# Slot tables of an edge-placing pass: the running sum on VectorE and bf16 parts in place of fp32 products

## The chip, the cores and the metric

One core of a Trainium2 chip runs the whole program; the other cores are idle. The metric is the device time of one execution in microseconds (us). TensorE (PE) multiplies matrices, VectorE (DVE) and ScalarE (ACT) work elementwise, GpSimd (POOL) issues the indirect transfers, SyncE (SP) the plain ones. Each engine runs its own list of instructions in order, and they meet through semaphores.

## The reference

The inputs are 6250 nodes with 128 features and 100000 edges, each with a source and a destination node. Two graph layers follow one another: an attention layer with 8 heads, whose softmax runs over the edges of one source node, and an edge MLP with a sum over the edges of each source; each is followed by a residual and a layer norm.

```python
q, k, v = x @ Wq.T + bq, x @ Wk.T + bk, x @ Wv.T + bv      # (6250, 8, 16)
scores  = sum(q[src] * k[dst], -1) / 4 + edge_attr_8
weights = softmax of scores over the edges with the same src
out     = segment_sum(v[src] * weights, dst) @ Wo.T + bo
x = layernorm(x + out)
h = silu(concat(x[src], x[dst], edge_attr_2) @ eW1 + eb1);  e = silu(h @ eW2 + eb2)
x = layernorm(x + silu(concat(x, segment_sum(e, src)) @ nW1 + nb1) @ nW2 + nb2)
```

## The kernel before

The nodes are cut into 49 windows of 128 lanes, so node n is lane n % 128 of window n / 128. The edges lie in 784 tiles of 128, one edge to a partition. Before anything is computed on them the edges are sorted by source: a first pass (`count_nodes`) counts the edges of each node, and the pass that the change touches (`place_and_project`) gives every edge its slot in a list padded by window and sends its record of 16 floats to that slot in DRAM. After it the records are read back (`load_records`), and scores, softmax, weighted sums, the projection, the edge MLP and the node MLP follow, one block after the other. Each block ends with all engines meeting.

The placing pass takes PG = 8 tiles at a time, 98 steps g in all, two (b = 0 and 1, doubly buffered) to an iteration i. For a step:

- `nodes` (DVE, helper line 229) makes 8 one-hots over the 128 lanes, `windows` (DVE, line 223) 8 one-hots over the WC = 50 window columns. Both are bf16 and are stored with the tile index innermost, so one tile's one-hot is read with a stride of 8 elements.
- `turn` (PE, L588) transposes the 8 lane one-hots, `turned` (ACT, L549 and L550) copies them out of PSUM twice, as bf16 and as fp32.
- `gram` (PE, L596) multiplies each transposed one-hot with itself: which edges of a tile share a lane. `earlier` (DVE, L459) masks this to the edges that come earlier in the tile.
- `count` (PE) builds the table of next free slots by lane and window, for each of the 8 tiles and for the one after them: L607 writes the running table 9 times by an fp32 product with the identity (450 columns), then L610 adds the one-hot counts of tile k to the tables k+1 to 8 (8 products of 400 down to 50 columns). `keep` (ACT, L541) copies it out.
- `slots_of` (PE) looks up each edge's entry: L622, an fp32 product of the turned one-hot with the kept table (50 columns, issued as two passes), and L623, a bf16 product that adds the earlier edges of the same tile.
- `finish` (DVE, L487 to L519) masks the result with the window one-hot (L487), sums it (L491), works out the row of the record in short operations on 8 columns (L495 to L517) and copies the record (L519). On b = 1 it also splits the projected q and v rows into three bf16 parts and stores them (L470 to L481).
- `send` (POOL, L652) issues 8 indirect transfers, one for each tile. `finish` waits for those of step g - 2 before it writes the same buffers (`s_sent`).
- On b = 0, `project` (PE, L580 and L581) makes one window's q, k and v rows: an fp32 product of a row of ones with the bias (384 columns, one row deep) and one of x with the weights.

The order on each engine is written out by hand. In step g, PE does slots(g), count(g+1), gram(g+1), project, turn(g+2). DVE does earlier(g+1), nodes(g+2), finish(g), windows(g+2). ACT does keep(g+1), the copies of the projection, turned(g+2). ACT first issues 20 transfers that zero the sums (L535).

## Time and profile before

| | us |
|---|---|
| median of 3 runs | 6396.11 (6384.83 to 6405.34) |
| the profiled execution | 6388.47 |
| its span, first to last instruction | 6386.7 |
| first record transfer of the placing pass starts | 189.73 |
| last one starts | 1488.43 |
| reading back starts | 1500.28 |

The placing pass is about a fifth of the span. Over the whole span PE is 63% busy, POOL 57%, DVE 37% and ACT 19%. Overlapping durations count once in a busy time. In a row of the timeline, the bracket holds how long the engine sat idle before the instruction and what ended that.

### The profile page before, as it was taken

The numbers are of one execution on the slowest core, as the hardware profiler recorded it, in microseconds if no ns is written. First come the engines' busy times: TensorE is split into PE (matmuls) and PEld (weight loads), VectorE is DVE, ScalarE is ACT, GpSimd is POOL, SyncE is SP. The second block draws the span as 40 slices with busy tenths as digits, with TensorE's granted clock in tenths as the row PEclk, the third lists the DMA queues.
The fourth block names the chain that finished last, engine by engine and source line by source line (L and its number), as shares of the span: only waits on it lengthen the run. The fifth ranks groups of instructions, "written<-read, shape, count | busy, mean of one in ns | idle before, by whom it ended". The sixth has DMA issues, their size and how long they took to land. (4 is left out here: it accounts for less than half of the span.)

```text
span 6386.7 us, 92237 instructions
## 1 busy us (share of the span) xinstructions
PE 4045.0 (63%) x25409; PEld 3223.8 (50%) x25410; DVE 2370.2 (37%) x6387; ACT 1207.9 (19%) x2083; POOL 3663.4 (57%) x3321
## 2 busy tenths in 40 slices
PE   6899998993433343322666566666255778877786
PEld 4566555552222222212555555555235667766674
DVE  6344434442222222258232222222243334343344
ACT  0222222220111110101111111111022333333332
POOL 0455555555666666631888888888404555555551
PEclk9555555555565555555777777777567888888888
DMA  2100000002111111100444444444511111111111
GB/s 111 54 10 10 10 10 10 10 10 68 43 42 44 43 41 44 42 22 4 36 35 35 35 36 35 35 36 36 104 58 34 37 37 37 38 37 37 37 37 53
DMA packets 278676, 238.39 MB, mean 37 GB/s; under 512 B 57255, under 2 KB 246759, under 8 KB 278246
## 3 DMA queue, kind: packets, MB, share of 16 engines
q0 software_dynamic: 198144, 170.19, 17.2%
q1 hardware_dynamic: 77604, 54.50, 2.8%
q10 hardware_dynamic: 2880, 13.11, 0.5%
q8 instruction: 25, 0.41, 0.0%
q14 instruction: 23, 0.18, 0.0%
HBM read 143.89 MB, written 93.71 MB: 37 GB/s over the span
## 5 line engine op out<-in xcount | busy, mean ns | idle before, releaser
L1075 POOL DMA_INDIRECT sums_dram<-we_merged_rows,we_idx x832 | 1286.3, 1546 | 477.8 <-DVE we_idx L1127 226.2
L1670 POOL DMA_INDIRECT ed_bg<-b_rows_dram,ed_idx x832 | 792.4, 952 | 669.8 <-DVE ed_idx L1678 442.3
L652 POOL DMA_INDIRECT records_dram<-rec_out,row_idx x784 | 768.0, 980 | 577.3 <-DVE rec_out L519 297.8
L751 POOL DMA_INDIRECT sc_k<-k_rows_dram,sc_idx x832 | 799.8, 961 | 470.4 <-issue 248.8
L1195 PE MATMUL ps_merged<-we_rows,we_same_dst 128*128 128x129 f32 x1664 | 359.3, 383 | 588.6 <-issue 429.5
L1195 PEld LDWEIGHTS ps_merged<-we_rows,we_same_dst 128*128 128x128 f32 x1664 | 307.8, 276 | 623.6 <-issue 613.8
L853 PE MATMUL ps_q<-tab,sc_oht 128*128 x2496 | 372.0, 263 | 373.5 <-issue 369.4
L1815 PE MATMUL ps_ed_s<-ed_ohf,ed_efs 128*128 128x128 f32 x1664 | 432.8, 417 | 188.6 <-ACT ed_efs L1755 126.4
L853 PEld LDWEIGHTS ps_q<-tab,sc_oht 128*128 128x128 bf16 x2496 | 249.8, 103 | 495.8 <-issue 442.1
L779 DVE TENSOR_TENSOR sc_prods<-ps_q,sc_k 128x1024 f32<-128x1024 f32 x104 | 127.2, 1223 | 925.9 <-remote 884.9
L1815 PEld LDWEIGHTS ps_ed_s<-ed_ohf,ed_efs 128*128 128x128 f32 x1664 | 335.8, 226 | 235.1 <-issue 193.2
L1114 DVE SCALAR_TENSOR_TENSOR we_firsts<-we_merged_rows,lane_unmark,two_marks 128x4 f32<-128x4 f32 x208 | 46.2, 222 | 1067.2 <-ACT we_merged_rows L1149 1067.2
L459 DVE TENSOR_TENSOR place_earlier<-ps_gram,tri 128x512 bf16<-128x512 f32 x196 | 126.2, 686 | 771.2 <-PE ps_gram L596 657.3
L622 PE MATMUL ps_slots<-place_table,place_oh_tf 128*128 128x50 f32 x1568 | 405.6, 408 | 0.0
L622 PEld LDWEIGHTS ps_slots<-place_table,place_oh_tf 128*128 128x128 f32 x1568 | 398.7, 328 | 0.6 <-issue 0.6
L1149 ACT ACTIVATE we_merged_rows<-ps_merged 128x516 f32<-128x516 f32 x208 | 125.0, 601 | 1288.9 <-DMA sums_dram<-we_merged_rows,we_idx 1274.2
L843 PE MATMUL ps_oht<-identb,sc_oh 128*128 128x128 bf16 x832 | 100.8, 286 | 415.4 <-ACT sc_oht L816 202.5
L1174 PE MATMUL ps_dst_row<-ident,we_dsts 128*128 128x128 f32 x1664 | 351.5, 383 | 0.0
L1693 DVE TENSOR_TENSOR ed_hs<-ps_z,ed_bg 128x512 f32<-128x512 f32 x208 | 143.5, 690 | 546.3 <-remote 429.7
L1174 PEld LDWEIGHTS ps_dst_row<-ident,we_dsts 128*128 128x128 f32 x1664 | 337.1, 299 | 0.0
L610 PE MATMUL ps_table<-place_ohw,place_oh 128*128 128x400 bf16 (+7 forms) x784 | 332.5, 582 | 0.0
L1707 DVE TENSOR_TENSOR vals<-vals,ps_ed_s 128x128 f32 x832 | 238.9, 287 | 193.1 <-issue 99.2
(288 smaller groups left out, 7736.7 us busy)
## 6 DMA issues: line engine op xcount, KB each, us to landing
sc_k<-k_rows_dram,sc_idx POOLq DMA_INDIRECT x832
sums_dram<-we_merged_rows,we_idx POOLq DMA_INDIRECT x832
ed_bg<-b_rows_dram,ed_idx POOLq DMA_INDIRECT x832
sums_dram<-zero_rows ACTq DMA_DIRECT2D x20, 640.0 KB, 8.5
records_dram<-rec_out,row_idx POOLq DMA_INDIRECT x784
co_rows<-sums_dram SPq DMA_DIRECT2D x48, 256.0 KB, 3.9
records_dram<-rfill SPq DMA_DIRECT2D x16, 416.0 KB, 6.9
records<-records_dram SPq DMA_DIRECT2D x1, 6656.0 KB, 18.5
```

What stands on the lines that cost most here:

```text
L610: ins = pe.matmul(table[:, k + 1:PG + 1, :], ohl[:, b, :, k], ohw[:, b, :, k].unsqueeze(1).to_broadcast([P, PG - k, WC]), start=False, sto ...
L622: pe.matmul(slots[b][:, k, :], ltf[:, b, k, :], kept[:, b, k, :], start=True, stop=False)
L652: pool.indirect_dma_start(c.rec_rows, bass.IndirectOffsetOnAxis(ap=idx[:, b, j:j + 1], axis=0), out[:, b, j, :], None, bounds_check=SLOTS ...
L751: pool.indirect_dma_start(kg[:, r, k * F:(k + 1) * F], None, c.k_dram[:, :], bass.IndirectOffsetOnAxis(ap=idx[:, r, k:k + 1], axis=0)).the ...
L853: ins = pe.matmul(psq[b][:, k * F:(k + 1) * F], oht[:, b, k, :], c.tab[:, j, bass.ds(win[k] * F, F)], start=(j == 0), stop=(j == 2))
L1075: pool.indirect_dma_start(c.acc_dram[k][:, :], bass.IndirectOffsetOnAxis(ap=idx[:, r, k:k + 1], axis=0), rows[:, r, k, 0:F], None, compute ...
L1174: ins = pe.matmul(psd[:, k * P:(k + 1) * P], dst[:, r, k:k + 1].to_broadcast([P, P]), c.ident[:, :], start=True, stop=True)
L1195: ins = pe.matmul(merged[b][:, k, 0:F + 1], same[:, b, k, :], con[:, b, k, :], start=True, stop=True)
L1670: pool.indirect_dma_start(bg[:, r, k * F:(k + 1) * F], None, c.b_dram[:, :], bass.IndirectOffsetOnAxis(ap=idx[:, r, k:k + 1], axis=0)).the ...
L1693: dve.tensor_tensor(h[:, b, :], psz[b][:, :], bg[:, r, :], ALU.add).then_inc(s_zs, 1)
L1707: dve.tensor_tensor(acc, acc, pss[r % 2][:, k * P:(k + 1) * P], ALU.add).then_inc(s_add, 1)
L1815: ins = pe.matmul(pss[b][:, k * P:(k + 1) * P], ef[:, b, k, :], ohf[:, b, :, k], start=True, stop=True)
```

## The change

- `keep` moves from ACT to DVE. PE no longer writes the running table: its count products start their own accumulation (`start=(k == 0)`, 400 columns instead of 450), and DVE adds the table before the step to the sums in PSUM (fp32, `kept`). DVE then splits the kept table into two bf16 parts (`kb`): a copy to bf16 and a subtraction.
- `slots_of` does two bf16 products with these parts in place of the fp32 one. ACT's fp32 copy of the turned one-hots is gone; the bf16 one is now doubly buffered.
- The window one-hots are stored tile by tile (contiguous blocks of 50), made by `blocks_onehot`; count and slots_of read them without a stride. They are made inside `finish`, right after the masking.
- The bias is split into three bf16 parts once, ahead of the loop (`bias_rows_of_qkv`), and added by one bf16 product of ones with a tile whose first three rows hold the parts. It is loaded to all partitions.
- The order: PE does count(g+1), gram(g+1), slots(g), project, turn(g+2); DVE does nodes(g+2), keep(g+1), earlier(g+1), finish(g) with windows(g+2) inside.

```diff
+def blocks_onehot(dve, c, e, t0, out):
+
+    return dve.tensor_tensor(out, c.iotab[:, 0:WC, 0].unsqueeze(1).to_broadcast([P, PG, WC]),
+                             e.hi[:, bass.ds(t0, PG)].unsqueeze(2).to_broadcast([P, PG, WC]), ALU.is_equal)
+
...
-        ohw = sb("place_ohw", [P, 2, WC, PG], BF16)
-        lt = sb("place_oh_t", [P, PG, P], BF16)
-        ltf = sb("place_oh_tf", [P, 2, PG, P], F32)
+        ohw = sb("place_ohw", [P, 2, PG, WC], BF16)
+        lt = sb("place_oh_t", [P, 2, PG, P], BF16)
+        kb = sb("place_table_parts", [P, 2, 2, PG, WC], BF16)
...
+        bias = sb("b_qkv", [P, 3 * F], F32)
+        bp = sb("b_qkv_parts", [P, 3, 3 * F], BF16)
+        bk = sb("b_qkv_rows", [P, 3 * F], BF16)
...
                 def windows(i, b):
                     g = 2 * i + b
+                    wait_count(dve, s_msk, g - 1)
+                    blocks_onehot(dve, c, e, g * PG, ohw[:, b]).then_inc(s_ohw, 1)
+
+                def keep(i, b):
+
+                    g = 2 * i + b
                     wait_count(dve, s_slots, g - 1)
-                    wait_count(dve, s_msk, g - 1)
-                    windows_onehot(dve, c, e, g * PG, ohw[:, b]).then_inc(s_ohw, 1)
+                    dve.wait_ge(s_hist, g + 1)
+                    wait_count(dve, s_tab, 2 * g)
+                    before = e.start[:, :] if isinstance(g, int) and g == 0 else kept[:, 1 - b, PG, :]
+                    dve.tensor_copy(kept[:, b, 0, :], before).then_inc(s_tab, 1)
+                    dve.tensor_tensor(kept[:, b, 1:PG + 1, :], pstab[:, 0:PG * WC].rearrange("p (k w) -> p k w", w=WC),
+                                      before.unsqueeze(1).to_broadcast([P, PG, WC]), ALU.add).then_inc(s_tab, 1)
+                    dve.wait_ge(s_tab, 2 * g + 2)
+                    dve.tensor_copy(kb[:, b, 0], kept[:, b, 0:PG, :]).then_inc(s_parts, 1)
+                    dve.wait_ge(s_parts, 2 * g + 1)
+                    dve.tensor_tensor(kb[:, b, 1], kept[:, b, 0:PG, :], kb[:, b, 0], ALU.subtract).then_inc(s_parts, 1)
...
                     g = 2 * i + b
                     win = i if b == 1 else None
                     dve.wait_ge(s_slots, g + 1)
-                    dve.tensor_tensor(own[:, :, :], slots[b], ohw[:, b].rearrange("p w k -> p k w"), ALU.mult).then_inc(s_msk, 1)
+                    dve.tensor_tensor(own[:, :, :], slots[b], ohw[:, b], ALU.mult).then_inc(s_msk, 1)
+                    dve.wait_ge(s_msk, g + 1)
+                    ahead, half, there = pair_at(i, b, 2)
+                    if there:
+                        windows(ahead, half)
                     if win is not None:
                         part(win, 0)
-                    dve.wait_ge(s_msk, g + 1)
                     dve.tensor_reduce(slot[:, :], own[:, :, :], AX_X, ALU.add).then_inc(s_red, 1)
...
                 def step(i, b):
-                    for by, work in ((1, earlier), (2, nodes), (0, finish), (2, windows)):
+                    for by, work in ((2, nodes), (1, keep), (1, earlier), (0, finish)):
                         at, half, there = pair_at(i, b, by)
                         if there:
                             work(at, half)
+                    if isinstance(i, int) and i == -1:
+                        windows(0, b)
+                    if isinstance(i, int) and i == -1 and b == 1:
+                        bias_rows_of_qkv()
+
+                def bias_rows_of_qkv():
+
+                    dve.wait_ge(s_w, 96)
+                    n = 0
+                    for j in range(3):
+                        dve.tensor_copy(bp[:, j, :], bias[:, :]).then_inc(s_bias, 1)
+                        n += 1
+                        dve.wait_ge(s_bias, n)
+                        if j < 2:
+                            dve.tensor_tensor(bias[:, :], bias[:, :], bp[:, j, :], ALU.subtract).then_inc(s_bias, 1)
+                            n += 1
+                            dve.wait_ge(s_bias, n)
+                    dve.tensor_scalar(bk[:, :], bp[:, 0, :], c.ident[:, 0:1], None, ALU.mult).then_inc(s_bias, 1)
+                    for j in (1, 2):
+                        n += 1
+                        dve.wait_ge(s_bias, n)
+                        dve.scalar_tensor_tensor(out=bk[:, :], in0=bp[:, j, :], scalar=c.ident[:, j:j + 1],
+                                                 in1=bk[:, :], op0=ALU.mult, op1=ALU.add).then_inc(s_bias, 1)
...
-                def keep(i, b):
-                    g = 2 * i + b
-                    wait_count(act, s_slots, g - 1)
-                    act.wait_ge(s_hist, g + 1)
-                    act.activation(kept[:, b].rearrange("p k w -> p (k w)"), pstab[:, 0:(PG + 1) * WC],
-                                   ACT.Copy).then_inc(s_tab, 1)
-
                 def turned(i, b):
                     g = 2 * i + b
                     act.wait_ge(s_tr, g + 1)
-                    wait_count(act, s_gram, g)
                     wait_count(act, s_slots, g - 1)
-                    act.activation(lt[:, :, :].rearrange("p k n -> p (k n)"), pst[:, :], ACT.Copy).then_inc(s_lt, 1)
-                    act.activation(ltf[:, b].rearrange("p k n -> p (k n)"), pst[:, :], ACT.Copy).then_inc(s_lt, 1)
+                    act.activation(lt[:, b].rearrange("p k n -> p (k n)"), pst[:, :], ACT.Copy).then_inc(s_lt, 1)
...
                 def project(win):
+                    pe.wait_ge(s_bias, 8)
                     pe.wait_ge(s_x, 16 * win + 16)
                     wait_count(pe, s_qv, win)
                     wait_count(pe, s_k, win)
-                    pe.matmul(psx[:, 0:3 * F], one[:, :], bias[:, :], start=True, stop=False)
+                    pe.matmul(psx[:, 0:3 * F], c.ones[:, :], bk[:, :], start=True, stop=False)
...
                 def count(i, b):
 
 
                     g = 2 * i + b
-                    table = pstab[:, 0:(PG + 1) * WC].rearrange("p (k w) -> p k w", w=WC)
-                    before = e.start[:, :] if isinstance(g, int) and g == 0 else kept[:, 1 - b, PG, :]
+                    table = pstab[:, 0:PG * WC].rearrange("p (k w) -> p k w", w=WC)
                     pe.wait_ge(s_ohw, g + 1)
-                    wait_count(pe, s_tab, g)
-                    pe.matmul(table, c.ident[:, :], before.unsqueeze(1).to_broadcast([P, PG + 1, WC]),
-                              start=True, stop=True)
+                    wait_count(pe, s_tab, 2 * g)
                     for k in range(PG):
-                        ins = pe.matmul(table[:, k + 1:PG + 1, :], ohl[:, b, :, k],
-                                        ohw[:, b, :, k].unsqueeze(1).to_broadcast([P, PG - k, WC]),
-                                        start=False, stop=True, skip_group_check=True)
+                        ins = pe.matmul(table[:, k:PG, :], ohl[:, b, :, k],
+                                        ohw[:, b, k, :].unsqueeze(1).to_broadcast([P, PG - k, WC]),
+                                        start=(k == 0), stop=True, skip_group_check=True)
                     ins.then_inc(s_hist, 1)
 
                 def slots_of(i, b):
                     g = 2 * i + b
                     pe.wait_ge(s_gm, g + 1)
-                    pe.wait_ge(s_tab, g + 1)
-                    pe.wait_ge(s_lt, 2 * g + 2)
+                    pe.wait_ge(s_parts, 2 * g + 2)
                     wait_count(pe, s_msk, g - 1)
                     for k in range(PG):
-                        pe.matmul(slots[b][:, k, :], ltf[:, b, k, :], kept[:, b, k, :], start=True, stop=False)
-                        ins = pe.matmul(slots[b][:, k, :], gm[:, b, k, :], ohw[:, b, :, k], start=False, stop=True)
+                        for j in range(2):
+                            pe.matmul(slots[b][:, k, :], lt[:, b, k, :], kb[:, b, j, k, :], start=(j == 0), stop=False)
+                        ins = pe.matmul(slots[b][:, k, :], gm[:, b, k, :], ohw[:, b, k, :], start=False, stop=True)
...
                 def step(i, b):
                     here = pair_at(i, b, 0)[2]
                     ahead, half, any_ahead = pair_at(i, b, 1)
                     later, later_half, any_later = pair_at(i, b, 2)
-                    if here:
-                        slots_of(i, b)
                     if any_ahead:
                         count(ahead, half)
                         gram(ahead, half)
+                    if here:
+                        slots_of(i, b)
                     if b == 0 and here:
                         project(i)
                     if any_later:
```

## Rows read from the trace of the kernel before

**Rows 1.** Busy time by engine; last are PE's granted clock, DMA share, GB/s.

```profile
400.00:800.00 400.00, 366.92 (x1565) 240.50 (x1565) 164.32 (x531) 83.77 (x135) 235.02 (x241) 0.51 0.05 10
```

**Rows 2.** The record copies on DVE: count, durations, first and last start.

```profile
L519 DVE COPY rec_out<-records x98: 217/227/232, 188.5 to 1474.4; 128x128 f32 x90, 128x128 f32<-128x128 f32 x8
```

**Rows 3.** Timeline of PE over one step: start, us, what ran.

```profile
811.17 1.07 PE L588 MATMUL ps_place_t<-identb,place_oh 128*128 128x128 bf16 x8 [2.06 <-DVE place_oh L229]
...
812.04 0.61 PE L622 MATMUL ps_slots<-place_table,place_oh_tf 128*128 128x50 f32 x2
...
816.13 1.82 PE L607 MATMUL ps_table<-place_table,ident 128*128 128x450 f32 x2
...
817.75 3.41 PE L610 MATMUL ps_table<-place_ohw,place_oh 128*128 128x400 bf16 x8
...
820.98 1.03 PE L596 MATMUL ps_gram<-place_oh_t 128*128 128x128 bf16 x8
...
821.94 1.64 PE L580 MATMUL ps_qkv<-b_qkv,one_row 1*128 1x384 f32 x2
...
823.52 1.65 PE L581 MATMUL ps_qkv<-w_qkv,xt 128*128 128x384 f32 x2
...
824.96 1.06 PE L588 MATMUL ps_place_t<-identb,place_oh 128*128 128x128 bf16 x8
```

**Rows 4.** Timeline of DVE: first and last instruction of two steps.

```profile
809.15 1.29 DVE L459 TENSOR_TENSOR place_earlier<-ps_gram,tri 128x512 bf16<-128x512 f32 x2 [8.69 <-PE ps_gram L596]
...
815.06 0.35 DVE L223 TENSOR_TENSOR place_ohw<-iota_by_tile,win_of 128x400 bf16<-128x400 bf16 x1
...
822.05 1.29 DVE L459 TENSOR_TENSOR place_earlier<-ps_gram,tri 128x512 bf16<-128x512 f32 x2 [6.63 <-PE ps_gram L596]
...
826.74 0.37 DVE L223 TENSOR_TENSOR place_ohw<-iota_by_tile,win_of 128x400 bf16<-128x400 bf16 x1
```

**Rows 5.** Timeline of POOL over its last 16 issues: first and last.

```profile
1469.30 0.97 POOL L652 DMA_INDIRECT records_dram<-rec_out,row_idx  x1 [1.95 <-issue]
...
1488.43 0.97 POOL L652 DMA_INDIRECT records_dram<-rec_out,row_idx  x1 [0.30 <-issue]
```

**Rows 6.** Transfers two us after that issue: DMA share and GB/s come last.

```profile
1491.00:1492.00 1.00, 0.00 (x0) 0.00 (x0) 0.00 (x0) 0.00 (x0) 0.00 (x0) 0.50 0.00 0
```

**Rows 7.** Groups of DVE in the stretch 400 to 2200, shapes kept apart.

```profile
L487 DVE TENSOR_TENSOR place_masked<-ps_slots,place_ohw 128x400 f32<-128x400 f32 x81 | 71.2, 878 | 2.8 <-PE ps_slots L623 2.8
...
L491 DVE TENSOR_REDUCE slot<-place_masked 128x8 f32<-128x400 f32 x81 | 45.9, 566 | 1.4
...
L470 DVE CAST qv_parts<-qv_rests 128x256 bf16<-128x256 f32 x82 | 23.5, 287 | 0.0
...
L475 DVE TENSOR_TENSOR qv_rests<-qv_rests,qv_parts 128x256 f32<-128x256 f32 x41 | 17.1, 417 | 0.0
...
L495 DVE CAST sloti<-slot 128x8 int32<-128x8 f32 x81 | 15.7, 194 | 1.4
```

**Rows 8.** Start of the pass: the timeline of ACT and POOL.

```profile
169.21 1.02 ACT L549 ACTIVATE place_oh_t<-ps_place_t 128x1024 bf16<-128x1024 bf16 x1 [64.12 <-issue]
...
189.73 1.22 POOL L652 DMA_INDIRECT records_dram<-rec_out,row_idx  x1 [45.65 <-DVE rec_out L519]
```

**Rows 9.** POOL's issues by group over the span; mean ns after the busy time.

```profile
L751 POOL DMA_INDIRECT sc_k<-k_rows_dram,sc_idx x832 | 799.8, 961 | 470.4 <-issue 248.8 <-DVE sc_idx L761 221.3 <-DVE sc_prods L779 0.3
...
L652 POOL DMA_INDIRECT records_dram<-rec_out,row_idx x784 | 768.0, 980 | 577.3 <-DVE rec_out L519 297.8 <-issue 279.5
```

**Rows 10.** Timeline of POOL and DVE where their instructions met.

```profile
397.20 0.68 DVE L229 TENSOR_TENSOR place_oh<-iota_by_tile,lane_of 128x1024 bf16<-128x1024 bf16 x1
397.25 1.48 POOL L652 DMA_INDIRECT records_dram<-rec_out,row_idx  x1 [0.30 <-issue]
...
1466.37 0.97 POOL L652 DMA_INDIRECT records_dram<-rec_out,row_idx  x1 [0.30 <-issue]
1466.89 0.45 DVE L495 CAST sloti<-slot 128x8 int32<-128x8 f32 x1
```

More of the change, by code:

```diff
@@ L401, in place_and_project @@
         w = sb("w_qkv", [P, 3 * F], F32)
-        bias = sb("b_qkv", [1, 3 * F], F32)
-        one = sb("one_row", [1, P], F32)
+        bias = sb("b_qkv", [P, 3 * F], F32)
+        bp = sb("b_qkv_parts", [P, 3, 3 * F], BF16)
+        bk = sb("b_qkv_rows", [P, 3 * F], BF16)
         xt = sb("xt", [P, P], F32)
@@ L560, in step @@
                 def step(i, b):
-                    ahead, half, there = pair_at(i, b, 1)
-                    if there:
-                        keep(ahead, half)
                     if b == 0 and (not isinstance(i, int) or 0 <= i < NW):
```

14 lines of the change are left out of this document (6 added, 8 removed).

## The prediction

> **What bounds the kernel now.** I read first the busy time of each engine in a stretch of the placing pass. PE is busy 367 of 400 us at a granted clock of 0.51, its lower level of 1.2 GHz, POOL 235, DVE 164 [rows 1]. The record copies on DVE give the pace: 98 of them, first to last (1474.4 - 188.5) / 97 = 13.26 us a step [rows 2]. The timeline of PE shows where this goes [rows 3]. A step with a projection is slots 4.09 us (812.04 to 816.13), the running table 1.62, count 3.23, gram 0.96, project 1.58 for the bias and 1.44 for x, turn 0.87: 13.8 us without a gap. A step without a projection has the first four and turn, and PE stands 2.06 us ahead of turn for the one-hots, which DVE makes only after it has had gram's result: 12.8. Their mean is the 13.3 of rows 2. So PE sets the pace, together with one hand-over to DVE in every second step. DVE waits 8.69 and 6.63 us for gram in the same two steps [rows 4], and a whole step of its own takes 6.26 us with the q and v parts and 5.06 without (first start to last end).
>
> The next limit is not DVE but POOL. Its last 16 issues stand back to back, with everything that they need long there: (1488.43 - 1469.30) / 15 = 1.275 us each, 0.97 of work and 0.30 of gap [rows 5]. A step has 8 of them, so POOL can't go below 10.20 us a step, 1000 us for the 784 issues. This is the number to compare all savings with.
>
> **PE, part by part.** The identity product goes: -1.62. Count keeps 1800 columns, which took 3.23 us with the stride (1.79 ns each); gram reads contiguous bf16 columns and takes 0.96 for 8 x 128 (0.94 ns each, loads and switch in it), so count costs 1.7. Slots go from 16 products (of which 8 in two passes) to 24 bf16 ones. Each needs a load of 128 columns; gram's pairs of load and product take 0.12, so 24 x 0.12 = 2.9 us; the upper bound is today's 4.09, as today too each tile has three loads. The bias goes from 1.58 to 384 x 0.94 ns = 0.36. New sum: 1.7 + 0.96 + 2.9 + 0.85 = 6.4, with a projection 8.2, mean 7.3 us. With slots and count not faster at all it is 4.09 + 3.23 + 0.96 + 0.85 + half of 1.8 = 10.0. At either end PE is under POOL's 10.20. The hand-over of 2.06 is gone too, as the lane one-hots are now the first thing in DVE's step.
>
> **ACT.** Two of its copies a step go. It waited for PE already, so this is worth nothing by itself; it lets go of gram and turn earlier.
>
> **DVE** gets work. keep is four instructions: a copy of 50 columns (at most the 0.23 of the record copy [rows 2], I take 0.2), an addition of 400 columns from PSUM (0.57 as the sum over 400 columns at L491, at most the 0.88 of L487, whose second input is strided), a copy to bf16 (0.29 for 256 columns at L470, 0.36 for 400), a subtraction (0.42 for 256 at L475, 0.57 for 400) [rows 7]: 1.7 us, at most 2.1. L487 loses its stride: 0.88 to 0.57, or no gain. The window one-hots were 0.36 us and now read one input with a stride and write 400 columns: 0.57 to 0.88, so +0.2 to +0.5, I take 0.35. Two steps: 6.26 + 5.06 + 2 x (1.7 - 0.3 + 0.35) = 14.8 us, bounds 14.3 and 16.6, against 20.4 at POOL. The order holds no circle that is longer: from the windows of g+1, PE needs 1.7 + 0.96 + 2.9 = 5.6 us to slots(g), while DVE has the rest of finish(g-1), nodes, keep and earlier to do, over 6 us, before it wants them.
>
> **POOL then sets the pace.** finish(g) waits for the transfers of step g - 2 before it writes the same buffers. After the last issue the transfers end within 2 us [rows 6], so the row indices of g are there some 8 us before POOL has done g - 1. DVE stands in this wait, and behind it stand the record copy, the tables and the one-hots of g+3, for which PE waits; but DVE needs 7.4 us from one such wait to the next and has 10.2. So POOL never starves, and PE and DVE idle.
>
> **Start and end.** Today ACT is held by its 20 issues and copies the first turned tiles at 169.21, and the first record goes at 189.73 [rows 8]. After: gram(0) as before, earlier(0) some 3.5 us behind that copy's start, to 172.7, windows(1) to 173.3, the bias rows on DVE (three copies of 384 columns at 0.36, two subtractions at 0.55, one product at 0.3, two fused operations at 0.55: 3.6 us with waits 3.9) to 177.2; nodes(2), keep(1), earlier(1), finish(0) take 0.7 + 1.7 + 1.3 + 3.2, PE's slots(0) are done at 178.3. The first record goes at about 185, 5 us earlier. The end is the same: reading back starts 10.9 us after the last issue ends.
>
> **POOL's price under load.** Today DVE works in large part while POOL waits. After, POOL never waits, so they meet more often. The trace shows both ways of it [rows 10]. L229, which reads two tensors from SBUF, began 0.05 us before an issue, and that issue took 1.48 in place of 0.97: it ended 0.85 after L229 had. A short cast that began 0.52 after an issue took 0.45, where the mean of its group is 0.19 [rows 7, 10], and ended with the issue. On average it is small: 980 ns against the usual 970 or so of rows 5; in the score pass, where POOL also runs in long stretches beside DVE, the like issues take 961 [rows 9]. After the change two steps hold, of operations with two inputs from SBUF, nodes 1.36, windows 1.2, the new subtraction 1.14, the rests of q and v 0.84 and six short fused ones 1.0, and of copies, casts and operations with a constant 0.4 + 0.72 + 1.4 + 0.46 + 0.87 + 0.57: 9.9 us in all, 4.95 a step. Today POOL meets chiefly L229, 0.68 a step, for about 8 x 9 ns. In proportion that is 0.07 x 4.95 / 0.68 = 0.5 us a step. Lower bound 0, upper bound all of the 4.95. I take 0.4: 10.6 us a step.
>
> The sum: 98 x 10.6 = 1039, from 185 to 1224, where 1489.4 stood: -265 us from the profiled execution's 6388.5, so 6123. That execution lies 7.6 us under the median of the runs shown, whose spread is 20 us; I say 6125. The floor, with nothing met, is 185 + 1000 = 1185: 6084. Changes under 0.3% (19 us) can't be told from none in this kernel.
>
> **The rivals.**
> *POOL is held up in part.* A third of DVE's 4.95 us a step lands on POOL: 11.8 us, 98 x 11.8 = 1156, -148: 6240. For it: DVE is released by POOL's own transfers, so its operations fall on a fixed phase, which may be a bad one. Against: the averages of rows 9.
> *DVE becomes the bound.* 19 short copies and operations in two steps, each lengthened by 0.26 as the one in rows 10, on the upper bound of 16.6: 21.5, 10.8 a step, -246: 6143. Against: the mean of 0.19 says how seldom it happens, though that is with POOL idle in part.
> *POOL is held up for all of it.* Every two-input operation, copy and cast of DVE stops the issue for its whole length: (20.4 + 9.9) / 2 = 15.1 us a step, 98 x 15.1 = 1480, +176: 6565. It decides from 3.06 us a step on, 0.38 on each issue; the worst single one in rows 10 is 0.51. Against: it needs nearly every operation to meet an issue at its sensitive moment.
> *PE and DVE in turn.* If count waited for windows and DVE for slots, a step would be 7.3 + 7.4 = 14.7 us: +139, 6530. The order above speaks against it.
> *The bf16 products and blocks are not faster.* PE at 10.0 stays hidden: 6125 as well.
>
> On holding up POOL the Trainium skill is stricter than the rows ("SBUF — State Buffer", Who interferes with whom): it calls the pair of ports that VectorE and GpSimd share an exclusive lock, taken for the whole instruction, by copies and casts in their two-port modes and by two-input operations against a GpSimd instruction that reads SBUF; the other side fully blocks. By that rule the third rival's 6565 is what would come; by the means, 980 ns against 970 undisturbed [rows 5, 9], it is 6125.
>
> **Chances.** POOL at 10.2 to 11.0: 0.68. Held up in part: 0.14. DVE the bound: 0.10. Held up in full 0.04, in turn 0.04. The first alone gives 6084 to 6165. For the range I add most of the second and the noise: 6080 to 6200. Faster 0.91, between 0.02, slower 0.07.
>
> **What would show it.** POOL: 0.30 us gaps marked as issue throughout, not waits for the record copy; 784 issues in 1000 to 1080 us, mean near 1.02 us. DVE idle ahead of the row index, for the transfers. PE's slots 2.9, count 1.7, bias 0.36 us, PE idle 30%. The forecast is wrong if POOL still waits for the record copy in every step, or if its mean goes over 1.15 us.

## The result

The changed kernel takes 6454.28 us (median of 4 runs, 6449.71 to 6467.23) where the kernel before takes 6400.73 on the same chip (4 runs, 6384.83 to 6406.03): ratio 1.0089, 95% interval 1.0076 to 1.0103. It is 54 us slower; 6125 was forecast. The profiled execution took 6454.73 us, 66 more than that of before. The placing pass holds nearly all of it: the last record transfer starts at 1547.0 where it was 1488.4 [rows 5].

The page's group of POOL's record transfers, to be set against L652 of before [rows 9], and the busy time of each engine in the stretch of rows 1:

```profile
L683 POOL DMA_INDIRECT records_dram<-rec_out,row_idx x784 | 797.7, 1017 | 718.4 <-DVE rec_out L543 481.6
```

```profile
400.00:800.00 400.00, 158.27 (x1393) 116.65 (x1391) 206.13 (x611) 36.48 (x70) 234.90 (x230) 0.57 0.05 10
```

PE fell from 367 of 400 us to 158, which is 5.5 us a step where 7.3 was forecast, and POOL's mean is 1017 ns, which is the forecast's. But POOL did no more in the stretch than before (234.90 us for 235), and over the pass it waited 481.6 us for the record copy in place of 297.8. No engine is busy for more than 59% of the time. The view of one line's instructions, for the transfers, gives the pace: from 183.2 to 1547.0, and without the last 7 issues (8.9 us) this is (1363.8 - 8.9) / 97 = 13.97 us a step. Worked out in the same way, before has 13.30.

```profile
L683 POOL DMA_INDIRECT records_dram<-rec_out,row_idx x784: 969/972/1602, 183.2 to 1547.0; - x196
```

**What a step looks like.** Timeline of POOL over one run of issues, and what follows it. Start, us, what ran; in brackets the idle time ahead and what ended it:

```profile
745.18 0.97 POOL L683 DMA_INDIRECT records_dram<-rec_out,row_idx  x1 [8.17 <-DVE rec_out L543]
746.45 0.97 POOL L683 DMA_INDIRECT records_dram<-rec_out,row_idx  x1 [0.30 <-issue]
...
754.91 0.97 POOL L683 DMA_INDIRECT records_dram<-rec_out,row_idx  x1 [0.30 <-issue]
756.19 1.34 POOL L683 DMA_INDIRECT records_dram<-rec_out,row_idx  x1 [0.30 <-issue]
...
765.49 0.97 POOL L683 DMA_INDIRECT records_dram<-rec_out,row_idx  x1 [0.30 <-issue]
772.83 0.97 POOL L683 DMA_INDIRECT records_dram<-rec_out,row_idx  x1 [6.36 <-DVE rec_out L543]
```

Sixteen issues, two steps' worth, without a gap, and then 6.4 us of nothing. PE's timeline over the same time, to be set against [rows 3]:

```profile
749.79 1.72 PE L642 MATMUL ps_table<-place_ohw,place_oh 128*128 128x400 bf16 x8 [3.33 <-DVE place_ohw L229]
751.35 1.04 PE L631 MATMUL ps_gram<-place_oh_t 128*128 128x128 bf16 x8
752.18 0.29 PE L654 MATMUL ps_slots<-place_table_parts,place_oh_t 128*128 128x50 bf16 x2
...
753.96 0.20 PE L654 MATMUL ps_slots<-place_table_parts,place_oh_t 128*128 128x50 bf16 x1 [0.66 <-issue]
755.39 0.20 PE L655 MATMUL ps_slots<-place_ohw,place_earlier 128*128 128x50 bf16 x1 [1.22 <-issue]
756.13 0.48 PE L615 MATMUL ps_qkv<-b_qkv_rows,ones 128*128 128x384 bf16 x1 [0.54 <-issue]
757.56 1.74 PE L616 MATMUL ps_qkv<-w_qkv,xt 128*128 128x384 f32 x2 [0.95 <-issue]
759.74 0.69 PE L623 MATMUL ps_place_t<-identb,place_oh 128*128 128x128 bf16 x5 [0.34 <-issue]
761.19 0.41 PE L623 MATMUL ps_place_t<-identb,place_oh 128*128 128x128 bf16 x2 [0.76 <-issue]
770.15 1.72 PE L642 MATMUL ps_table<-place_ohw,place_oh 128*128 128x400 bf16 x8 [8.55 <-DVE place_ohw L229]
```

and DVE's, which waits for PE's results:

```profile
754.79 0.19 DVE L465 COPY place_table<-place_table 128x50 f32<-128x50 f32 x1 [1.03 <-remote]
754.89 0.57 DVE L466 TENSOR_TENSOR place_table<-ps_table,place_table 128x400 f32<-128x400 f32 x1
755.50 0.58 DVE L469 CAST place_table_parts<-place_table 128x400 bf16<-128x400 f32 x1
756.11 0.57 DVE L471 TENSOR_TENSOR place_table_parts<-place_table,place_table_parts 128x400 bf16<-128x400 f32 x1
759.97 1.29 DVE L480 TENSOR_TENSOR place_earlier<-ps_gram,tri 128x512 bf16<-128x512 f32 x2 [3.28 <-remote]
768.39 0.57 DVE L508 TENSOR_TENSOR place_masked<-ps_slots,place_ohw 128x400 f32<-128x400 f32 x1 [7.13 <-remote]
769.15 0.86 DVE L229 TENSOR_TENSOR place_ohw<-iota_by_tile,win_of 128x400 bf16<-128x400 bf16 x1 [0.19 <-DVE place_masked L508]
```

Read the three together. For the first 8 us of POOL's run PE works as it should: count 1.72, gram 1.04, products of slots every 0.04 us. From 753.1 on its work comes in single products and short bursts, at about the pace of POOL's issues, with gaps marked as issue, so with nothing awaited that the profile shows. And its results are announced late, from the first issues on. The turned one-hots end at 746.45, and ACT, idle since 741.52, starts to copy them 3.8 us later:

```profile
750.27 1.02 ACT L588 ACTIVATE place_oh_t<-ps_place_t 128x1024 bf16<-128x1024 bf16 x1 [8.75 <-remote]
```

Later in the run it is worse: gram's last product ended at 752.39, yet L480, for which DVE was free at 756.68, starts at 759.97; the last product of slots ended at 755.59, yet L508 starts at 768.39, 12.8 us later and 1.9 us after POOL's last issue ended. The profile calls that releaser "remote": it finds no event in this core's records that ended the wait. DVE's instructions that wait only for DVE (L466, L469, L471) follow one another without delay at the same time. So what is held up is PE and its signals, and DVE and ACT by waiting for them. In the stretch 400 to 1200 most of DVE's waits (total us, times, longest) are of this kind; the one other of weight is L465's, 33.9 us in 4 times, marked as issue:

```profile
DVE place_masked L508 <- remote: 135.7, 30, 12.6
DVE place_table L465 <- remote: 90.7, 19, 15.2
DVE place_earlier L480 <- remote: 85.1, 21, 6.2
```

### The profile page after: what moved, and what is told of

Its sections match the earlier page's. It is cut to its first block and busy times, and to the rows that moved or that the text cites. A ratio compares the mean times of both kernels' runs of the same rounds, so it can differ in the third digit from the quotient of the medians.

```text
span 6453.0 us, 91860 instructions
## 1 busy us (share of the span) xinstructions
PE 3392.1 (53%) x25164; PEld 2848.6 (44%) x25165; DVE 2552.7 (40%) x6787; ACT 1061.8 (16%) x1887; POOL 3694.7 (57%) x3320
## 5 line engine op out<-in xcount | busy, mean ns | idle before, releaser
L683 POOL DMA_INDIRECT records_dram<-rec_out,row_idx x784 | 797.7, 1017 | 718.4 <-DVE rec_out L543 481.6
L642 PE MATMUL ps_table<-place_ohw,place_oh 128*128 128x400 bf16 (+7 forms) x784 | 157.9, 375 | 438.2 <-DVE place_ohw L229 389.0
L642 PEld LDWEIGHTS ps_table<-place_ohw,place_oh 128*128 128x128 bf16 x784 | 109.7, 161 | 501.0 <-issue 435.8
L874 PEld LDWEIGHTS ps_oht<-identb,sc_oh 128*128 128x128 bf16 x832 | 80.4, 158 | 504.3 <-issue 336.4
L1818 PE MATMUL ps_z<-tab,ed_oht 128*128 x2496 | 268.5, 232 | 60.6 <-issue 59.9
```

The source lines that it names most:

```text
L642: ins = pe.matmul(table[:, k:PG, :], ohl[:, b, :, k], ohw[:, b, k, :].unsqueeze(1).to_broadcast([P, PG - k, WC]), start=(k == 0), stop=Tru ...
L683: pool.indirect_dma_start(c.rec_rows, bass.IndirectOffsetOnAxis(ap=idx[:, b, j:j + 1], axis=0), out[:, b, j, :], None, bounds_check=SLOTS ...
L874: ins = pe.transpose(pst[:, k * P:(k + 1) * P], oh[:, r % 2, :, k], c.identb[:, :])
L1818: ins = pe.matmul(z, oht[:, b, k, :], c.tab[:, j, bass.ds(win[k] * F, F)], start=False, stop=(j == 2))
```

## The experiments

Theory 1 came out of these rows: unbroken issuing on POOL holds PE up. Its rival, theory 2: the steps hang together in a way that needs 13.9 us. All times a step below are worked out as above, from the first and last start of the transfers, and each ratio is to the kernel before on the same chip.

**A pause after each eight: with work, and by waiting.**

```diff
                     for j in range(PG):
                         pool.indirect_dma_start(...)
+                    pool.memset(rest[:, :], 0.0).then_inc(s_rest, 1)   # pause8: rest is 128x2600 f32
+                    pool.wait_ge(s_sent[b], 16 * PG * (i + 1))         # landed8, in place of the memset
```

In pause8 and its like POOL waits for the memset (s_rest) ahead of its next eight.

> The changed kernel with a memset on GpSimd (128x2600 f32, about 2.3 us by the 2.07 us of a 128x2350 one in the trace) behind each eight transfers. Theory 1, unbroken issuing holds the other engines up: the changed kernel's placing takes (1547.0 - 183.2) / 98 = 13.9 us per step of eight because after eight transfers GpSimd goes straight on with the next eight, and TensorE's, VectorE's and ScalarE's work then stands still for the second half of that run. A pause after each eight keeps the runs short: 8 x 1.275 + 2.4 = 12.6 us per step, 6454 - 98 x 1.3 = about 6327 us (6290 to 6400). Theory 2, the steps depend on each other so that 13.9 us is what the chain of one step needs whatever GpSimd does: the pause is added or hidden, 6454 to 6680 us.

> The changed kernel with GpSimd waiting behind each eight transfers until they have landed (about 2 us after the last issue, nothing executed on GpSimd meanwhile). Theory 1 (unbroken issuing holds the others up): as with the memset, about 12.3 us per step, 6300 to 6400 us. Theory 2 (chain of one step): 6454 us or more. A third possibility, that the memset's own traffic or lock matters, shows as a difference between this and the memset version of over 30 us.

pause8: 6414.38 us, ratio 1.0022 (1.0009 to 1.0035), 13.49 us a step. landed8: 6321.97, ratio 0.9862 (0.9840 to 0.9884), 12.52 a step. The wait that only takes time away from POOL makes the changed kernel faster than before, by 1.4%. With it the picture is the one that was forecast: DVE no longer waits for PE at all, but for POOL's transfers ahead of the row index:

```profile
DVE row_idx L541 <- DMA records_dram<-rec_out,row_idx: 302.6, 64, 6.8
```

pause8 lost only by its length: POOL stands 3.2 us between eights (memset 2.29, and the wait for its end) where landed8 stands 2.1 to 2.4, and with 8 x 1.00 of issues and 7 x 0.30 of gaps that is all of its step. Its forecast of 12.6 counted the memset without that wait. That settles the third possibility in landed8's text: the two differ by 92 us, and a pause longer by 1 us, 98 times, is as much.

**Half of the transfers, and ten in place of eight.**

```diff
-                    for j in range(PG):
+                    for j in range(PG // 2):        # half_sent, on the changed kernel
```

```diff
+                    for j in (6, 7):                # before_ten, on the kernel before
+                        pool.indirect_dma_start(c.spare_rows, ... idx[:, b, j:j + 1] ..., out[:, b, j, :], ...)
```

> The changed kernel with only the first four of each eight record transfers (half the records are left out, so later stages read rows that were never placed). Everything else of a step stays. Theory 1: GpSimd needs 5.1 us per step, pauses after each four, and nothing is held up; the step is set by VectorE's 7.4 us or TensorE's, 7.5 to 9 us, placing 735 to 880 us, 5820 to 5970 us in all. Theory 2: 13.9 us per step stays, 6400 us or more. Between the two: the hold-up goes with the number of transfers and not with their unbroken run, about 10 us per step, 6070 us.

> The kernel before with ten transfers per step: the last two of each eight are sent once more, to a spare tensor of the same size. GpSimd then has 10 x 1.275 = 12.75 us of the step's 13.26. Theory 1: GpSimd's pauses go, TensorE's work is held up as in the changed kernel and the step becomes 14.5 to 16.5 us, 6520 to 6720 us. Theory 2, nothing is held up by the issuing: the two transfers fit into GpSimd's 3.1 us of idle time per step, 6401 to 6430 us.

half_sent: 5864.68 us, ratio 0.9156 (0.9134 to 0.9178), 7.88 us a step; DVE is busy 358 of 400 us and sets it. The rival is refuted: the chain of steps can go at 7.9, and PE and DVE need no more than this. But PE's signals are late here too, with four issues in a row and 2.7 to 4 us of pause behind them. Timelines of PE, DVE and ACT in half_sent; POOL's four issues run from 602.17 to 606.97:

```profile
603.32 0.22 PE L655 MATMUL ps_slots<-place_ohw,place_earlier 128*128 128x50 bf16 x1
603.65 1.36 PE L616 MATMUL ps_qkv<-w_qkv,xt 128*128 128x384 f32 x2
606.52 0.57 DVE L508 TENSOR_TENSOR place_masked<-ps_slots,place_ohw 128x400 f32<-128x400 f32 x1 [0.84 <-remote]
608.04 0.28 ACT L593 ACTIVATE qv_rows<-ps_qkv 128x128 f32<-128x128 f32 x1 [6.60 <-remote]
```

Each comes 3.0 us after the last product that it waits for (603.54 and 605.01). So theory 1's "nothing is held up" fails in this detail: the lateness starts within the first issues, and costs little here because DVE is busy till 605.69 anyway.

before_ten: 6840.34 us, ratio 1.0679 (1.0655 to 1.0704), and (1922.8 - 188.7 - 8.9) / 97 = 17.8 us a step. Two more issues, for which POOL had 3.1 us of idle time, cost the kernel before 4.5 us a step, more than the 1 to 3 expected: POOL now runs 20 issues without a gap, and then idles 10.6 us. The same hold-up, without any part of the change. In one place the kernel before has it by itself: sixteen issues nearly in a row (2.3 us between the first and the second), and then

```profile
965.62 0.97 POOL L652 DMA_INDIRECT records_dram<-rec_out,row_idx  x1 [8.06 <-DVE rec_out L519]
```

**How short a pause will do.** These are pause8's edit with other sizes and places of the memset, as their texts say.

> The changed kernel with a memset of one column on GpSimd behind each eight transfers. In the run with the 2600-column memset GpSimd went 3.2 us between two eights, 0.9 us over the memset's 2.29, so this pause should be about 1.0 us. Theory 1a, the hold-up clears in any pause of GpSimd's transfers, however short: 10.2 + 0.7 = 10.9 us per step, 6322 - 98 x 1.5 = 6175 us (6150 to 6230). Theory 1b, about 2 us of pause are needed for 10 us of issuing (a backlog that drains at a rate): part of the hold-up comes back, 12.5 to 14 us per step, 6320 to 6470 us.

> The changed kernel with a memset of one column on GpSimd behind each four transfers, so two pauses of about 1.0 us in a step. Theory 1a (any pause clears it): 10.2 + 1.4 = 11.6 us per step, about 6245 us (6220 to 6290), slower than one pause per eight. Theory 1b (a backlog that drains at a rate): two short pauses do what one of 2 us does, also about 6245 us, and then faster than one pause per eight.

> The changed kernel with a memset of 740 columns (about 0.65 us) on GpSimd behind each eight transfers and the wait for it, so about 1.6 us of pause, between the 1.1 us that let the hold-up come back every fourth or fifth step and the 2.2 us with which it never came. Theory 1b, a backlog that grows while GpSimd issues and drains in its pauses, some 12 us of the chip's time for eight transfers whoever pays: 12.2 to 12.5 us per step, as fast as either (ratio to before 0.986 to 0.992). Theory 1c, the threshold lies below 1.6 us: 10.2 + 1.3 = 11.5 us per step, 90 us less than with the landing wait, ratio 0.972.

> The changed kernel with a one-column memset and the wait for it behind each four transfers: two pauses of 1.1 us in a step, 11.8 us of GpSimd's time per step. Theory 1b (backlog drained by the sum of the pauses): no hold-up, 11.8 to 12.4 us per step, ratio 0.977 to 0.986. Rival, what clears it is the length of one pause, not their sum: hold-ups as with one pause of 1.1 us, 13 us per step or more, ratio 0.995 or more.

tiny8: ratio 0.9913 (0.9896 to 0.9929), 12.63 us a step. Its pauses were 1.1 us, and in each fourth or fifth step POOL still idled some 7 us, so 1a fell. tiny4: 0.9914 (0.9897 to 0.9931), but it isn't what its text says: a memset among the issues cost POOL no gap, only the wait for it at the end did, so it repeats tiny8. pause16 (memset 128x740, gap 1.7): 0.9838 (0.9822 to 0.9855), 12.3 us a step, and as in landed8 DVE waits for the transfers and no longer for PE. two_pauses: 0.9837 (0.9815 to 0.9860), 12.2 us a step: POOL hardly starves, but the hold-up isn't gone. From 400 to 800 DVE still waits 102.8 us in 28 of some 33 steps for the product of slots (longest 6.5).

Is 12.2 a pace that the chip sets, as theory 1b has it ("some 12 us of the chip's time whoever pays")? The rows don't ask for it. In pause16 an issue takes 1046 ns in the mean, and 8 x 1.046 + 7 x 0.30 + 1.7 = 12.2: POOL's own work, gaps and pause. two_pauses gives 8 x 1.020 + 6 x 0.30 + 2 x 1.0 = 12.0, with a few longer stops, and landed8 8 x 1.008 + 7 x 0.30 + 2.2 = 12.4. On a chip where the gathers are not held up at all (score_pause, below) the same placing pass takes 12.37, no less. The 11.5 of theory 1c counted undisturbed issues; with the longer ones it comes to 12.2 too, so pause16 doesn't decide between the two. What does speak for something that piles up and drains is tiny8, where the hold-up comes back only each fourth or fifth step. What fills wasn't seen, and its rate isn't known.

**What in the issuing does it.**

```diff
-   idx[:, b, j:j + 1] ... out[:, b, j, :]
+   idx[0:64, b, j:j + 1] ... out[0:64, b, j, :]                 # rows64: half of the rows of each transfer
```

```diff
-                    for j in range(PG):
-                        pool.indirect_dma_start(...)
+                    for j in range(PG // 2):                                    # memsets: no transfers at all;
+                        ins = pool.memset(rest[:, j * 1040:(j + 1) * 1040], 0.0)   # twice a step, and a wait in between
```

> The changed kernel with each record transfer over 64 of the 128 partitions (half of the records are left out, later stages read rows that were never placed); eight transfers per step as before. Theory A, what piles up is what a transfer writes (descriptors, one per row): half of it per transfer, no hold-up, and the step is GpSimd's 10.2 us if an issue still lasts 0.97 us, less if it gets shorter: 8 to 10.3 us per step, 5885 to 6110 us. Theory B, it is GpSimd's being busy with issuing, whatever it writes: if an issue still lasts 0.97 us the step stays at 13.9 us, 6450 us.

> The changed kernel with each of the eight record transfers of a step replaced by a memset of 128x1040 f32 (0.95 us each, as long as a transfer's 0.97); no record is placed, so later stages read rows that were never written. GpSimd is as unbroken as before. Theory 1 as it is about transfers: other engines aren't held up, and the step is GpSimd's 8 x 1.3 = 10 us or a little over, 10 to 11 us, 6090 to 6170 us. Rival, any unbroken work of GpSimd holds the others up (the port that it shares with VectorE): 13.5 us or more per step, 6400 us or more.

rows64: 6501.05 us, ratio 1.0157 (1.0137 to 1.0177), 14.3 us a step, more than the 13.9 of theory B. An issue still lasts 902 ns, and runs of 16 are mostly followed by 8 to 10 us of idle time. So it isn't the amount of rows or bytes; theory A fell. memsets: 6169.55, ratio 0.9695 (0.9676 to 0.9715), 10.1 us a step, POOL busy for 300 of 400 us. The time by itself doesn't refute the rival: DVE sets this step (380 of 400 us busy), POOL waits 1.5 to 3.6 us for it behind each eight, and pauses like these ended the hold-up with transfers too. What refutes it are the signals. PE and ACT while POOL runs eight memsets from 599.59 to 607.27, with 0.15 us in their middle:

```profile
600.48 1.48 PE L617 MATMUL ps_qkv<-w_qkv,xt 128*128 128x384 f32 x2
602.09 0.28 ACT L594 ACTIVATE qv_rows<-ps_qkv 128x128 f32<-128x128 f32 x1 [11.51 <-PE ps_qkv L617]
```

0.13 us after the product, where half_sent's four transfers made it 3.0. So it isn't POOL's work as such; it takes transfers. What memsets do to DVE is another thing, told at the end.

Transfers aren't enough either. The pass of the weighted sums adds rows to the sums in DRAM by 832 indirect transfers, and each keeps POOL for 1.55 us. The view of one line's instructions, in the kernel before and in bias_pause (a chip of the other kind, below):

```profile
L1075 POOL DMA_INDIRECT sums_dram<-we_merged_rows,we_idx x832: 1543/1547/1717, 3014.6 to 4552.8; - x167
L1099 POOL DMA_INDIRECT sums_dram<-we_merged_rows,we_idx x832: 1543/1547/1721, 2735.4 to 4273.4; - x167
```

In the kernel before all 832 stand in a row with no stop, 1.85 us each, for 1538 us. No wait of DVE, ACT or PE in 3100 to 3900 is marked as remote, and the pass takes as long on the other kind of chip. So issuing without a pause costs nothing at 1.85 us a transfer; in the placing pass it does at 1.275. These transfers differ in more than the pace (they add, their rows are longer, and each waits until the one four before it has landed), and so it isn't shown that the pace decides.

**One part of the change alone.**

> The kernel before with the bias by the bf16 product alone. It saves TensorE 1.58 - 0.35 = 1.2 us per two steps, 0.6 us per step. If TensorE still sets the step and GpSimd still pauses after each eight (2.3 us and more): 12.65 us per step, 60 us less, ratio 0.990. If the shorter step already lets GpSimd run two eights together: pairs as in the changed kernel now and then, 13.3 us or more, ratio 1.000 or more.

> The kernel before with the bias edit and with the pause of 740 columns and its wait (1.7 us) behind each eight transfers. If the hold-up is what ate the gain of the bias edit alone: TensorE's 12.65 us per step shows, 60 us less than before, ratio 0.990. If the bias edit saves nothing on the chip whatever GpSimd does: ratio 1.000. The whole change with the same pause had 0.984, so the other edits would be worth 0.4 us per step beside it.

> The kernel before with the same wait for the landing behind each eight transfers that took the changed kernel to 6322 us. Theory 1: TensorE's 13.26 us set its step and GpSimd pauses anyway (2.3 to 5.1 us), so the wait lies in idle time: 6385 to 6410 us. Rival, the wait itself gives something whatever the kernel (as the order of transfers and other traffic): about 80 us less, 6320 us.

bias_only: ratio 1.0027 (1.0009 to 1.0045), 13.35 us a step. Not faster, though PE's busy time in the stretch of rows 1 fell from 367 to 332. The timeline of POOL shows where the gain goes. In most steps POOL pauses 1.5 to 3.5 us, as it does with PE setting the pace, and then PE is early enough once for two eights to join, or to stand only 1.2 us apart, and a stop of 7 to 8 us follows:

```profile
610.13 0.97 POOL L673 DMA_INDIRECT records_dram<-rec_out,row_idx  x1 [2.48 <-DVE rec_out L520]
...
629.47 0.97 POOL L673 DMA_INDIRECT records_dram<-rec_out,row_idx  x1 [0.30 <-issue]
638.70 0.97 POOL L673 DMA_INDIRECT records_dram<-rec_out,row_idx  x1 [8.26 <-DVE rec_out L520]
```

With the pause of pause16 the same edit has ratio 0.9920 (0.9903 to 0.9937) and 12.72 us a step, the expected 12.65; but that run was on a chip of the other kind (below). Whether it was the pause or the chip that let the gain through isn't shown, nor what the remaining edits add beside it (0.9838). before_landed: 1.0021 (1.0011 to 1.0031), 13.27 us a step. The wait by itself gives nothing.

**Another kind of chip.** The last six runs were three more kernels (bias_pause, mixed, score_pause) and three repeats. Four of the six met chips that differ.

```diff
-                    for j in range(PG):
+                    for j in range(PG // 2):
                         pool.indirect_dma_start(...)
+                        ins = pool.memset(rest[:, j * 1300:(j + 1) * 1300], 0.0)   # mixed, mixed2
```

> The changed kernel with four of each eight transfers replaced by memsets of 128x1300 f32 (1.2 us), a transfer and a memset in turn (half of the records are left out, later stages read rows never placed). GpSimd has about 10 us of work per step, as in the changed kernel, and no pause. Theory A, what holds the others up is an unbroken run of GpSimd in which transfers are issued, however densely: 13 to 14 us per step, 6370 to 6460 us. Theory B, transfers add a backlog that drains at some 1.5 us each, so 2.5 us per transfer leaves it empty: GpSimd's 10 us sets the step, 10 to 10.8 us, 6070 to 6150 us.

> The same kernel (transfer and memset in turn, four of each eight transfers, half of the records left out) on another chip. Where before takes 6365 to 6405 us: theory A, any unbroken run in which transfers are issued holds the others up: 13 us per step or more, 6350 us or more. Theory B, a backlog that drains at about 1.5 us per transfer: 11.1 us per step as on the first chip, no idle time of over 4 us, 6150 to 6200 us (ratio 0.965 to 0.972).

> The changed kernel with the 740-column pause behind each eight record transfers and, new, behind each eight gathers of the score stage (832 gathers, now 24 unbroken in 30.2 us and 6.5 us idle, 1.53 us per gather). Pauses make it (8 x 1.24 + 1.4) / 8 = 1.42 to 1.5 us per gather. If the score stage is held up in the same way and pays more than the pauses cost: 25 to 90 us less than with the record pauses alone, ratio 0.970 to 0.980. If some 1.5 us per transfer is the rate that the chip lets through either way: no more than 20 us, ratio 0.981 to 0.986.

> The changed kernel once more, as it is. The kernel before's time on the same chip says which state it is. Where before takes about 5730 us (nothing is held up): GpSimd sets the step at 8 x 1.275 + 0.4 = 10.6 us as predicted, 2.6 us less than before's 13.26, 98 x 2.6 = 255 us less: 5475 us, ratio 0.955 (0.95 to 0.965). If the placing stage is held up even there: ratio 1.00 to 1.01. Where before takes 6365 to 6405 us: ratio 1.009 as measured, and the first question stays open.

> The changed kernel as it is, on another chip. Where before takes about 5730 us: 5475 us, ratio 0.955 (0.95 to 0.965), if the prediction's arithmetic holds without the hold-up; 1.00 to 1.01 if placing is held up even there. Where before takes 6365 to 6405 us: ratio 1.009 again.

The seven sets of experiments ran on seven chips. On two of them, that of mixed, bias_pause and score_pause and that of mixed2, the kernel before takes 5731.28 and 5734.64 us; on the others 6365 to 6406. The gathers of the score pass show where the time goes. The view of one line's instructions, in bias_pause, where that pass is as in the kernel before:

```profile
L775 POOL DMA_INDIRECT sc_k<-k_rows_dram,sc_idx x832: 940/944/1472, 1463.7 to 2517.9; - x167
its engine sat idle before it (us, times) until:
  issue: 253.3, 831
  DVE sc_idx L785: 1.1, 1
```

All 832 without a stop, (2517.9 - 1463.7) / 831 = 1.27 us each, where the kernel before on the first chip took 1.53 and waited 221.3 us for DVE [rows 9]. The edge pass gains 413 us in the same way (4537.0 to 5575.4, for 4817.4 to 6269.2). There the gathers aren't held up, however long POOL issues. score_pause: ratio 1.0091 (1.0075 to 1.0108) there. Its pauses among the gathers only cost, 1.44 us a gather for 1.27, and its question wasn't answered. Its placing pass, pause16's to the letter, takes 12.37 us a step (184.3 to 1393.5), and ACT gets PE's signals there within 0.2 us. mixed and mixed2: 0.9666 and 0.9669, 11.2 us a step, set by DVE (378 of 400 us busy), which the memsets slow down; so the 10 to 10.8 us of theory B in mixed's text, by which POOL would set the step, were not met. Both fell on this kind of chip, so for record transfers less densely laid it stays open whether they hold PE up. The changed kernel itself I never met there: again had before at 6393.02 and ratio 1.0096 (1.0077 to 1.0114), again2 had 6368.57 and 1.0026 (1.0017 to 1.0036), where POOL mostly ran 24 issues without a gap and then idled 7 to 11 us. So on five chips of the first kind before takes 6365 to 6406, but the changed kernel's ratio isn't the same on all of them, and ratios of different chips, those of the pauses too, can't be compared closer than about 0.7%.

## Why the prediction was wrong

**The step that failed** is "So POOL never starves, and PE and DVE idle", with the pace of 10.6 us that rests on it. It took for granted that PE does its work in the time that it takes with POOL pausing. POOL starved: 481.6 us of waits for the record copy, because PE's signals come late while POOL issues and its products all but stop after some 8 us of it. The size: 98 x (13.97 - 10.6) = 330 us, and 6454 - 6125 = 329. The only other terms of the sum, the start and the end, were off by 2 us and by 0.1 (reading back starts at 1558.8). The prediction's sign of being wrong, a wait for the record copy in every step, didn't come as it says: with two eights in a row it came in every second one, 47 times. Nor did its other sign, a mean issue over 1.15 us.

**The floor of 10.20.** The last 16 issues, 1.275 us each [rows 5], were right as a cadence and untested as a pace beside PE's work: they were read at the end of the pass, where no PE work was left that could be held up. With PE's work beside it and no pause a step took 13.97. The least with transfers was 12.2, and its pauses are in that.

**PE's parts** came out better than said. From one start to the next, as the prediction counts, count is 1.56 us (1.7 forecast), gram 0.83 (0.96), slots 0.9 (2.9), and the bias 0.29 in half_sent (0.36). Slots were the term that was too careful. The prediction took 0.12 for each load and product from gram's, but these 50-column products follow each other every 0.04 us at a granted clock of 0.50 (744.9 to 745.4). The granted clock in the stretch rose from 0.51 to 0.57.

**DVE's parts.** In landed8 DVE is busy 232.60 us in 400 to 800, 7.28 us a step of 12.5 (7.4 forecast). In the groups of the changed kernel keep's four take 0.20, 0.57, 0.42 and 0.58 us, L508 0.57, as forecast, and the window one-hots 0.86, near the upper bound of 0.88. (The bounds of 14.3 and 16.6 for two steps come out at 14.5 and 16.5 from the prediction's own terms, which changes nothing.) The groups in 400 to 1200:

```profile
L508 DVE TENSOR_TENSOR place_masked<-ps_slots,place_ohw 128x400 f32<-128x400 f32 x56 | 31.9, 569 | 135.7 <-remote 135.7
L229 DVE TENSOR_TENSOR place_ohw<-iota_by_tile,win_of 128x400 bf16<-128x400 bf16 x56 | 48.0, 856 | 10.7 <-DVE place_masked L508 7.8 <-issue 2.9
```

**The start.** First transfer at 183.2; 185 was forecast, 189.73 before.

**POOL's price under load.** 1017 ns in the mean, 972 undisturbed: 8 x 0.045 = 0.36 us a step, 0.4 forecast. In part that is luck, as POOL stood idle for a third of the pass; where it doesn't, in pause16, the mean is 1046, 0.6 us a step. The rival by which POOL would be held up in full is refuted: it would have made 15.1 us a step by way of long issues, and the issues aren't long. As the prediction reads the rule of the Trainium skill ("SBUF — State Buffer", Who interferes with whom), it falls with it as a price for these transfers. The section itself is milder on this point: it infers that two-input operations don't stall GpSimd's making of descriptors. What made the kernel slower was in no rival. "PE and DVE in turn" has the nearest step, 14.7, but half_sent's 7.88 shows that they aren't in turn.

**What stood in the rows.** The group of the score pass in rows 9 was read for its mean of 961 ns alone. The same row has 221.3 us of waits for DVE in a pass that has little else than POOL's issues to wait for. The same group in the view of one line's instructions, and two of its issues in the timeline, in the kernel before:

```profile
L751 POOL DMA_INDIRECT sc_k<-k_rows_dram,sc_idx x832: 938/944/1399, 1521.1 to 2789.3; - x167
```

```profile
1863.73 0.94 POOL L751 DMA_INDIRECT sc_k<-k_rows_dram,sc_idx  x1 [4.37 <-DVE sc_idx L761]
...
1900.13 0.94 POOL L751 DMA_INDIRECT sc_k<-k_rows_dram,sc_idx  x1 [6.31 <-DVE sc_idx L761]
```

(2789.3 - 1521.1) / 831 = 1.53 us a gather, though each 0.94 us one can follow the last within 0.30: 24 in a row, then 6.3 us of nothing. That looks like what the change brought into the placing pass, and the other kind of chip has neither the stops nor the 1.53; before_ten shows that two issues more a step would have been enough.

**What is shown and what isn't.** Shown on the first kind of chip: while POOL issues these transfers at 1.275 us each, PE's signals come late (by 3 us even with four issues in a row), and runs of 16 and more cost more time than they save (after, before_ten, rows64, again, again2). A pause of 1.7 to 2.4 us behind each eight takes PE off DVE's waits and gives ratios of 0.984 to 0.986, where the changed kernel has 1.003 to 1.010. It needs transfers, not memsets, and not their bytes. Not shown: which part of the chip PE and POOL share here, whether the pace or the sort of transfer spares the pass of the weighted sums, why two chips don't have it in the gathers, and whether the changed kernel would take about 5475 us there, as its arithmetic says.

## What to carry to other kernels

Don't take an engine's cadence in an undisturbed stretch for its sustained pace: look for a stage in which it already works without pauses beside the same kind of work, and divide its length by the count. When the work that made GpSimd pause gets shorter, put a short pause back (here the wait for the eight transfers to land) before judging the edit. And compare on one chip only: the kernel before differs by 10% between them, and pauses among the gathers, meant to help where they stall, only cost time on a chip where they don't.

## What the runs showed of the hardware

PE's signals come late while GpSimd issues indirect transfers at 1.275 us each without a gap, by 3.0 us in half_sent and by 12.8 in the step shown first. With memsets they don't (0.13), and at 1.85 us each, in the weighted sums, transfers without a gap cost nothing that the pass's length shows. The kernel before runs 10% faster on 2 of 7 chips, where the gathers of the score pass don't stop. GpSimd's memsets, on the other hand, lengthen DVE's copies and casts, far more than transfers do. Groups of the kernel with memsets, 400 to 1100:

```profile
L466 DVE COPY place_table<-place_table 128x50 f32<-128x50 f32 x69 | 120.9, 1753 | 0.0
L467 DVE TENSOR_TENSOR place_table<-ps_table,place_table 128x400 f32<-128x400 f32 x69 | 114.4, 1658 | 0.0
...
L470 DVE CAST place_table_parts<-place_table 128x400 bf16<-128x400 f32 x69 | 83.2, 1205 | 3.9
```

Beside transfers the copy takes 0.25, the addition 0.56 and the cast 0.40 (landed8). The addition starts 0.1 us after the copy and ends with it, so its length may be the copy's. The subtraction, with two inputs from SBUF, takes 575 ns in both runs. This fits the lock between VectorE and GpSimd that the Trainium skill describes ("SBUF — State Buffer", Who interferes with whom), in which copies and casts take part and two-input operations don't against an instruction that only writes. The window one-hots cost 0.86 us with a strided input and rows of 50, for 0.36 before.
